# A selective-scan kernel: sums of two scan steps in two array quadrants, issued as pairs; other load and step buffers

## The reference

```python
xs = _cross_scan(x)                       # 4 directions k, 192 channels d, L positions
dt = softplus(dts + dt_projs_bias)
def step(h, inp):                         # h: (B, 4, 192, 16 states)
    dtt, ut, bt, ct = inp
    dA = jnp.exp(dtt[..., None] * A)
    h = h * dA + (dtt * ut)[..., None] * bt[:, :, None, :]
    y = jnp.einsum('bkdn,bkn->bkd', h, ct)
    return (h, y)
...
y = _cross_merge(ys + Ds * u)             # the four directions added up
```

## Time and profile before

| | us |
|---|---|
| median of 3 runs | 12530.81 (12523.07 to 12570.84) |
| the profiled execution, its own time | 12556.06 |
| its span | 12554.3 |
| PE, DVE, ACT, POOL busy | 9985.9, 8321.4, 4365.6, 7736.3 |

### The profile page before, as it was taken

The page is one execution under the profiler, slowest core; times in us unless marked ns, Lnnn a source line. Parts: engine busy times, 40 slices in busy tenths (PEclk is TensorE's granted clock), DMA queues, the critical chain, the costliest instruction groups (busy, mean ns, idle before and its releaser), DMA issues. The chain is left out here.

```text
span 12554.3 us, 91878 instructions
## 1 busy us (share of the span) xinstructions
PE 9985.9 (80%) x28440; PEld 2877.6 (23%) x28440; DVE 8321.4 (66%) x7943; ACT 4365.6 (35%) x5374; POOL 7736.3 (62%) x3710
## 2 busy tenths in 40 slices
PE   6787877878778787878878778787878878778787
PEld 1112222122222212122122222212122122222212
DVE  2367666667666667666667666667666767667666
ACT  1243333424334233333423334243333423334243
POOL 0384766837567474766847567484766847567583
PEclk9697878879788787888979788887878979788897
DMA  0352542524335242542524335152543524345252
GB/s 14 90 123 63 125 106 69 123 67 118 86 93 138 49 119 63 122 110 69 123 68 114 88 93 138 49 119 63 125 106 73 124 67 116 83 97 134 56 122 56
DMA packets 358663, 1181.05 MB, mean 94 GB/s; under 512 B 67483, under 2 KB 68747, under 8 KB 358023
## 3 DMA queue, kind: packets, MB, share of 16 engines
q1 hardware_dynamic: 331703, 1157.28, 37.0%
q10 hardware_dynamic: 24800, 15.62, 0.5%
q0 software_dynamic: 1520, 0.78, 0.0%
HBM read 1004.06 MB, written 156.02 MB: 92 GB/s over the span
## 5 line engine op out<-in xcount | busy, mean ns | idle before, releaser
L1234 POOL TENSOR_TENSOR arena<-arena 128x1024 f32<-128x1024 f32 x1536 | 3666.8, 2401 | 734.6 <-issue 712.3
L1250 POOL TENSOR_TENSOR arena<-arena 128x1024 f32<-128x1024 f32 x1152 | 2713.9, 2356 | 1414.1 <-DVE arena L1189 1411.7
L1015 PE MATMUL ps<-arena,sel_y 128*32 128x512 f32 x6144 | 3307.6, 673 | 231.2 <-POOL arena L1250 208.7
L1189 DVE TENSOR_TENSOR_SCAN arena<-ps,arena 128x1024 f32<-128x1024 f32 x1152 | 2630.2, 2283 | 773.4 <-ACT ps L1127 711.9
L1127 ACT ACTIVATE ps<-arena,v_na 128x1024 f32<-128x1024 f32 x1536 | 1716.3, 1117 | 3461.1 <-DVE arena L1189 2214.7
L917 DVE TENSOR_REDUCE arena<-ps 128x1 bf16<-128x512 f32 x1632 | 1115.0, 683 | 1259.2 <-PE ps L700 1259.2
L1015 PEld LDWEIGHTS ps<-arena,sel_y 128*32 128x32 f32 x6144 | 601.3, 118 | 2420.0 <-issue 2046.6
L869 ACT ACTIVATE arena<-ps 128x512 f32<-128x512 f32 x1632 | 879.7, 591 | 774.5 <-PE ps L725 774.1
L725 PE MATMUL ps<-arena 33*128 33x512 f32 x3264 | 988.2, 684 | 111.7 <-ACT arena L869 85.7
L1179 DVE TENSOR_TENSOR_SCAN ps<-ps,arena 128x1024 f32<-128x1024 f32 x384 | 878.0, 2286 | 297.0 <-ACT ps L1127 289.2
L700 PE MATMUL ps<-arena 32*128 32x512 bf16 x1632 | 678.6, 416 | 476.8 <-DVE arena L917 476.0
(11 more groups left out here) (217 smaller groups left out, 12005.8 us busy)
## 6 DMA issues: line engine op xcount, KB each, us to landing
arena<-scan_dtu SPq DMA_DIRECT2D x770, 512.0 KB, 6.1
arena<-scan_dt SPq DMA_DIRECT2D x770, 512.0 KB, 4.7
arena<-scan_bc SPq DMA_DIRECT2D x260, 512.0 KB, 6.9
scan_dt<-arena SPq DMA_DIRECT2D x68, 512.0 KB, 8.1
scan_dtu<-arena SPq DMA_DIRECT2D x68, 512.0 KB, 4.8
scan_dt<-arena SPq DMA_DIRECT2D x68, 256.0 KB, 4.1
scan_dtu<-arena SPq DMA_DIRECT2D x68, 256.0 KB, 4.7
XN<-arena SPq DMA_DIRECT2D x204, 64.0 KB, 4.3
```

The costliest lines, as they stand in the source:

```text
L1015: mm = nc.tensor.matmul(ps[3][32 * q:32 * q + 32, HALF * h:HALF * h + HALF], sel_y[:, r, :], step[:, i % NBUF, HALF * h:HALF * h + HALF], ...
L1189: nc.vector.tensor_tensor_scan(step[:, i % NBUF, o], ps[2][:, o], step[:, i % NBUF, o], 0.0, ALU.mult, ALU.add).then_inc(m_h, 1)
L1234: pool.tensor_tensor(step[:, i % NBUF, :], dur[:, i // 2 % DUR, :], Bb[2 * (k // 2) + f], ALU.mult).then_inc(m_bu, 1)
L1250: pool.tensor_tensor(step[:, i % NBUF, :], step[:, i % NBUF, :], Cb[2 * (k // 2) + f], ALU.mult).then_inc(m_hcp, 1)
```

## The change

The step list is reordered: q runs inside f in pairs, so that steps 2p and 2p+1 have the same f and r and neighbouring quadrants q. The sums are issued for two steps at once, at the end of each odd step, behind both slots. A spread load now serves steps i and i+2, so loads are issued two at a time, every fourth step each, into four buffers for dt and four for dt*u; step buffers go from 10 to 8, and the arena grows by 512 words. From the second head pair on, front slots move back by one (87 to 88, 84 to 85, 119 to 120, and all from 156 on).

```diff
-        DTR, DUR, NBUF, LEAD = 2, 3, 10, 3
+        NDT, NBUF, LEAD = 4, 8, 3
...
-        MAX_ROWS = [49, 84, 119]
-        UNIT = [[52 + 2 * k for k in range(16)], [87 + 2 * k for k in range(16)], [122 + 4 * k // 3 for k in range(16)]]
+        MAX_ROWS = [49, 85, 120]
+        UNIT = [[52 + 2 * k for k in range(16)], [88 + 2 * k for k in range(16)], [123 + 4 * k // 3 for k in range(16)]]
...
-                if hs == 170:
+                if hs == 171:
                     norm_act(act, 1, (128, 128))
...
                 for r in range(2):
-                    for q in range(4 if c == 0 else 2):
+                    for p in range(0, 4 if c == 0 else 2, 2):
                         for f in range(2):
-                            STEPS.append((g, k, 8 * c + 2 * q + r, q, r, f))
+                            for q in (p, p + 1):
+                                STEPS.append((g, k, 8 * c + 2 * q + r, q, r, f))
...
+                two = (2 * p, 2 * p + 1)
+                wait_products(pe, two[1])
...
                 for h in range(2):
-                    mm = nc.tensor.matmul(ps[3][32 * q:32 * q + 32, HALF * h:HALF * h + HALF], sel_y[:, r, :],
...
-                mm.then_inc(m_y, 1)
+                    for i in two:
+                        _, _, _, q, r, _ = STEPS[i]
+                        mm = nc.tensor.matmul(ps[3][32 * q:32 * q + 32, HALF * h:HALF * h + HALF], sel_y[:, r, :],
...
+                mm.then_inc(m_y, 2)
 
             for i in range(NSTEP):
                 next(front)
-                if i >= 2:
-                    sums(i - 2)
                 next(front)
+                if i % 2 == 1 and i >= 3:
+                    sums((i - 3) // 2)
...
-                if i % 2 == 0:
-                    if i + 2 * DUR < NSTEP:
-                        sp.wait_ge(m_bu, i + 2)
-                        spread_du(sp, b, i + 2 * DUR, m_dul[i // 2 % DUR])
-                    if i + 2 * DTR < NSTEP:
+                n, at = i // 4, i % 4
+                if at in (1, 3) and 4 * n + 8 < NSTEP:
+                    for e in range(2):
+                        to = load_of(4 * n + 8 + e) % NDT
+                        if at == 1:
+                            sp.wait_ge(m_bu, 4 * n + 3 + e)
+                            spread_du(sp, b, 4 * n + 8 + e, m_dul[to])
+                        else:
+                            sp.wait_ge(m_da, 4 * n + 3 + e)
+                            spread_dt(sp, b, 4 * n + 8 + e, m_dtl[to])
...
-                    if i == GROUP_END[g_] + 2:
+                    if i == GROUP_END[g_] + 3:
                         taken(g_)
```

More of the change, by code:

```diff
@@ L161, in build @@
         g_t = sb("g_t", [128, 2, 4])
-        WORDS = 38400
+        WORDS = 38912
         arena = sb("arena", [128, WORDS])
@@ L945, in build @@
         m_cb = [sem(f"scan_c_block_loaded_{k}") for k in range(K)]
-        m_dtl = [sem(f"scan_dt_block_loaded_{i}") for i in range(DTR)]
-        m_dul = [sem(f"scan_dtu_block_loaded_{i}") for i in range(DUR)]
+        m_dtl = [sem(f"scan_dt_block_loaded_{i}") for i in range(NDT)]
+        m_dul = [sem(f"scan_dtu_block_loaded_{i}") for i in range(NDT)]
         m_ya = sem("scan_source_loaded")
@@ L965, in build, with load_of, loaded @@
         m_x = sem("scan_added")
-        def du_loads(m):
-            return sum(q % DUR == m % DUR for q in range(2, m + 1))
+        def load_of(i):
+            return 2 * (i // 4) + i % 2
+        def loaded(n):
+            return 16 * sum(q % NDT == n % NDT for q in range(2, n + 1))
         STEPS = []
@@ L1007, in scan_pe, with sums @@
         def scan_pe(pe, front):
-            def sums(i):
-                g, _, _, q, r, _ = STEPS[i]
-                wait_products(pe, i)
-                if g > 0 and i == GROUP_END[g - 1] + 1:
+            def sums(p):
+                two = (2 * p, 2 * p + 1)
+                wait_products(pe, two[1])
+                g = STEPS[two[0]][0]
+                if g > 0 and two[0] == GROUP_END[g - 1] + 1:
                     pe.wait_ge(m_ev, g)
                 for h in range(2):
-                    mm = nc.tensor.matmul(ps[3][32 * q:32 * q + 32, HALF * h:HALF * h + HALF], sel_y[:, r, :],
-                                          step[:, i % NBUF, HALF * h:HALF * h + HALF],
-                                          start=not any(st[0] == g and st[3] == q for st in STEPS[:i]),
-                                          stop=not any(st[0] == g and st[3] == q for st in STEPS[i + 1:]))
-                mm.then_inc(m_y, 1)
+                    for i in two:
+                        _, _, _, q, r, _ = STEPS[i]
+                        mm = nc.tensor.matmul(ps[3][32 * q:32 * q + 32, HALF * h:HALF * h + HALF], sel_y[:, r, :],
+                                              step[:, i % NBUF, HALF * h:HALF * h + HALF],
+                                              start=not any(st[0] == g and st[3] == q for st in STEPS[:i]),
+                                              stop=not any(st[0] == g and st[3] == q for st in STEPS[i + 1:]))
+                mm.then_inc(m_y, 2)
             for i in range(NSTEP):
                 next(front)
-                if i >= 2:
-                    sums(i - 2)
                 next(front)
+                if i % 2 == 1 and i >= 3:
+                    sums((i - 3) // 2)
             pe.wait_ge(m_cl, 6)
             keep_clock(14, bank(3))
-            for i in range(NSTEP - 2, NSTEP):
-                sums(i)
+            sums(NSTEP // 2 - 1)
             keep_clock(5, bank(3))
@@ L1056, in spread_dt @@
             _, k, j, _, _, _ = STEPS[i]
-            sp.dma_start(dtr[:, i // 2 % DTR, :], dt_d[image, k, 16 * j:16 * j + 16, :].unsqueeze(1).to_broadcast(
+            sp.dma_start(dtr[:, load_of(i) % NDT, :], dt_d[image, k, 16 * j:16 * j + 16, :].unsqueeze(1).to_broadcast(
                 [16, 8, L])).then_inc(done, 16)
@@ L1061, in spread_du @@
             _, k, j, _, _, _ = STEPS[i]
-            sp.dma_start(dur[:, i // 2 % DUR, :], du_d[image, k, 16 * j:16 * j + 16, :].unsqueeze(1).to_broadcast(
+            sp.dma_start(dur[load_of(i) % NDT], du_d[image, k, 16 * j:16 * j + 16, :].unsqueeze(1).to_broadcast(
                 [16, 8, L])).then_inc(done, 16)
@@ L1072, in ahead @@
             load_image(sp, after)
-            for i in (0, 2):
+            for i in (0, 1):
                 spread_du(sp, image, i, p_du)
@@ L1126, in decay @@
                 at = 24 * k + 2 * j + f
-                nc.scalar.activation(ps[2][:], dtr[:, i // 2 % DTR, :], ACT.Exp,
+                nc.scalar.activation(ps[2][:], dtr[:, n % NDT, :], ACT.Exp,
                                      scale=v_na[:, at:at + 1]).then_inc(m_da, 1)
@@ L1229, in state_input @@
                     pool.wait_ge(p_b, 32 * b + 32)
-                if i // 2 >= 2:
-                    pool.wait_ge(m_dul[i // 2 % DUR], 16 * du_loads(i // 2))
+                n = load_of(i)
+                if n >= 2:
+                    pool.wait_ge(m_dul[n % NDT], loaded(n))
                 if k:
                     pool.wait_ge(m_bl[k], 32)
-                pool.tensor_tensor(step[:, i % NBUF, :], dur[:, i // 2 % DUR, :], Bb[2 * (k // 2) + f],
+                pool.tensor_tensor(step[:, i % NBUF, :], dur[n % NDT], Bb[2 * (k // 2) + f],
                                    ALU.mult).then_inc(m_bu, 1)
```

49 lines of the change are left out of this document (26 added, 23 removed).

## The result

| | before | after |
|---|---|---|
| median of 5 runs, us | 12538.31 (12523.07 to 12584.47) | 12642.77 (12627.96 to 12655.48) |
| profiled execution, its span | 12554.3 | 12652.5 |
| PE, DVE, ACT, POOL busy | 9985.9, 8321.4, 4365.6, 7736.3 | 9452.8, 8181.4, 4355.4, 7661.8 |
| granted clock, mean of the span | 0.839 | 0.754 |

The ratio is 1.008, with a 95% interval of 1.0063 to 1.0097: slower, by less than 1%, where 12,330 (0.984) was forecast. All four engines have less to do and the kernel takes 104 us more.

The account below looks back on a forecast made before the run. It took a 5.41 us loop of PE with one trip through DVE, sums between the rough products, to bound score steps. Terms sum to -12.5 us an image, times 16 -200: 12,330, own range 12,180 to 12,460, with rivals 12,050 to 12,590.

Parts of the forecast that it names:

- Slots one later: Last stage: the next image's norm on ACT goes behind a decay, which stops waiting for POOL; -3 us an image (-6 to +2).
- The clock term in steps 8 to 19: Less PE work brings 1.2 GHz stretches; one half-clock step in four, +3 us an image; bounds none and two of four.
- The pattern term: Steps 9 to 19: the pair stands with the projection ahead of R1, the first rough product, while DVE waits; +3 an image.
- Rival D: Granted clock falls to 1.2 GHz in steps 9 to 19 and 42 to 57; +11 an image, 12,705; chance 11%.
- Steps 42 to 57: Loop gains only -2.5 us as DVE's path is next; half-clock steps add +4.5, per image.
- Steps 24 to 42: Sums behind both rough products save 15 us, joined maxima add 2, half-clock steps unchanged: -13 an image, between -21 and -4.
- The pair costs one step's price: Sums of two steps in different quadrants cost PE 1.84 us, one step's price, saving 1.84 in two steps.
- rival B: The second quadrant starts one pass late, +9 us an image on PE-bound steps; 12,475; chance 7%.
- rival E: The pair runs one after the other, 3.67 us behind the second rough product; +12 an image, 12,725; chance 4%.
- The pairs in steps 61 to 73: Two steps take 8.62 us, 0.77 less each; limited by busy POOL to -4.5 an image, between -5.8 and -1.
- Eight step buffers: POOL's input of step i+8 needs the sums of i; +0.7 at most at step 92's input, 0 elsewhere.
- Rival A: The clock holds and stage two loses its half-clock steps as well; -31 us an image, 12,035; chance 11%.

Follow-up runs that it names:

- e1: The changed kernel with the six dt projections back in even slots 176 to 186; 12408.51 us, ratio to before 0.9876.
- e3: The changed kernel with short bf16 products of zeros added between the two slots in steps 9 to 23; 12473.9 us, ratio 0.9929.
- e6: The kernel before with half of the sums left out, order, waits and slots unchanged; 12805.9 us from two runs, ratio 1.0188.
- e7: The changed kernel with dt slots back, zero products in steps 9 to 23 and in odd steps of 25 to 57 (without 35 and 51); 11925.81 us, ratio 0.9484.
- e4: The changed kernel with the sums of one step issued behind both slots of each step, instead of pairs; 12570.97 us, ratio 1.0017.
- e5: The kernel before with eight step buffers instead of ten, nothing else (part of its output wrong); 12553.03 us, ratio 0.999.

## Why the prediction was wrong

The forecast by stage, against what was measured, us per image:

| steps | forecast | measured | cause as the runs show it |
|---|---|---|---|
| 0–8 | 0 | -0.2 | |
| 8–19 | +6 | +13.0 | clock, mis-sized |
| 19–24 | 0 | +2.5 | clock, left out |
| 24–42 | -13 | -17.5 | the place of the sums |
| 42–57 | +2 | +1.9 | two errors that cancel |
| 57–61 | 0 | -0.1 | |
| 61–79 | -4.5 | -8.8 | pairs -4.3; slots one later at step 79 -4.5, not foreseen |
| 79–95 | -3 | +13.8 | dt slots, step failed |
| rest | 0 | +1.6 | |
| sum | -12.5 | +6.2 | (the period gives +5.8, over 15 distances) |

**The step that failed: "Slots one later".** The part looked at one operation that the shift moves, the norm of the next image, and closed with "DVE's own path stays". The shift moves the six dt projections with their linear part, clamp and exponential as well, and on ACT each of them goes from ahead of a decay to behind it, so that linear part and clamp, which ran ahead of and beside the decay, now come after it on the way to the next scan. Forecast -3 in a range of -6 to +2, measured +13.8 in steps 79 to 95; with the 4.5 that the same shift brought at step 79, which the prediction did not see either, the term is +9.3. e1 puts 12.5 of it (49.3 - 36.8) down to that one line. The remaining 3.7 in steps 88 to 95 lie between scans 88 and 90 (14.5 in e1, 12.3 before), where a pair stands between the projections on PE, and between scans 93 and 95 (10.5 against 8.5), with a clock that is at 1.2 GHz for 80% of the stage against 13% before; no run separated these. This step alone turns the sign: without the shift of the dt slots the change gives 12408.51, where the forecast less this term is 12,330 + 16 x 3 = 12,378.

**The clock term in steps 8 to 19 had the right sign and a quarter of the size.** The prediction took one half-clock step in four in steps 9 to 19, +3, with two in four as the bound. The records show 61% of the time, and e3 prices it at 11.7. The pattern term beside it (+3) was not too small: with the clock mostly back the stage takes 57.4 against 56.1. The prediction read the clock of a stage from PE's busy share, but its own had two stages at 87% busy, one with a clock of 0.94 and one with 0.81. Rival D named this stage and its condition, a clock under 0.8 in steps 8 to 24 (it is 0.67), and its 12,705 is 62 us from the median. That nearness is luck: its other half did not come true, since steps 42 to 59 stayed at 0.81, and it has no term for the dt slots, without which the kernel is faster than before. The argument against D, "at half clock PE fills up", is what e6 refutes: PE was busy for 70.49 of 72.00 us and the clock was at 0.57 all the same.

**Steps 42 to 57: +2 forecast, +1.9 measured, for other reasons.** The join of the half maxima at step 57 hardly waits for POOL any more (6.1 less), so pattern and clock together cost 8. e7 gives 7.3 of it back with fillers. A term that comes out right says little while its parts are not seen.

**Steps 24 to 42** took 93.1 where the forecast for the mean is 97.6 (110.6 - 13): 4.5 more were gained, although the time at 1.2 GHz rose from 28% to 42%, where it was taken to stay. The two joins of this stage, priced at 3.65 each, take 4.7 together before and 1.2 after. In the image of the earlier trace rows the window went from 117.5 to 93.0, where "near 105" was named. The part that the prediction did not separate is e4's: it is moving the sums that helps in this stage, and halving them costs 4.4.

**What held.** The pair costs one step's price (1.91; 3.51 to 3.63 at 1.2 GHz), against rival B's 2.3 and rival E's 3.6. The Trainium skill's rule on the strict order of small matmuls (TensorE: Matmul & The Clock Gate, Part 3), weighed in the prediction, does not hold for two column quadrants with all 128 rows: by it the pair would take 2.3. But the prediction read the Part one-sidedly: its table of measured speedups has tiles beside each other in columns overlap (three of 32 columns, 2.38 times as fast), and the 1.91 agrees with that. The pairs in steps 61 to 73 brought 4.3 where -4.5 was taken for steps 61 to 79. Eight step buffers cost nothing in the order of before (e5); with the pairs POOL's input waits 2.4 us an image for sums, where +0.7 was the bound, and what that costs is open. Rival A was right only that a held clock is worth some hundred microseconds: with the clock put back by fillers and the dt slots in place e7 took 11,926, under A's 12,035.

## What to carry to other kernels

When a change takes work off TensorE, ask first what the granted clock does in that stage: here half of the sums left out cost 1.9%, and products of zeros in the gaps took 1.3% off the kernel after. When a list of slots is moved, walk every operation that hangs on it past the waiting instructions of its own queue: with two slots a step and the waiting instruction between them, an odd shift puts what stood ahead of it behind it. Here, by the trace, that won 4.5 us an image at step 79, and it lost 12.5 in the dt part (e1). And look into any row whose mean is far from what its size asks for, before moving it about: 3649 ns for 16 elements a partition was the cheapest gain of the case.
